# Feed-forward merging on three pairs of PSUM banks: products in groups of three instead of two

## What is computed

```python
g = mean over tokens of (relu(x @ gate_w1.T + gate_b1) @ gate_w2.T + gate_b2)     # (32, 8)
mW1 = W1 + einsum('be,efh->bfh', g, TW1)       # (32, 1024, 256): one merged matrix per batch
mW2 = W2 + einsum('be,ehf->bhf', g, TW2)       # (32, 256, 1024)
u = gelu(einsum('bsh,bfh->bsf', x, mW1) + mb1)
out = einsum('bsf,bhf->bsh', u, mW2) + mb2
x_res = x_res + tanh(g_ffn[0]) * out
```

## Time and profile before

| | |
|---|---|
| time, median of 3 runs | 1381.49 us (1380.21 to 1385.34) |
| the profiled execution: its own time | 1387.4 us |
| the profiled execution: its span | 1385.6 us |
| mean granted TensorE clock | 0.971 |
| PE busy over the span | 1304.1 us (94%) |
| DVE, ACT, POOL busy | 968.4, 678.4, 528.1 us |
| the eight chunks of stage 2 | about 154 to 518 us of the span |

### The profile page before, as it was taken

One profiled execution on the slowest core, in us unless ns is written; L12 is line 12 of the kernel. 1 busy time (PEld: TensorE's weight loads), 2 busy tenths in 40 slices (PEclk: granted clock), 3 DMA queues, 4 the chain that ended last, 5 costly groups with the idle time before them and its releaser, 6 DMA issues. The chain is left out here.

```text
span 1385.6 us, 32665 instructions
## 1 busy us (share of the span) xinstructions
PE 1304.1 (94%) x12672; PEld 924.2 (67%) x12672; DVE 968.4 (70%) x1641; ACT 678.4 (49%) x1447; POOL 528.1 (38%) x781
## 2 busy tenths in 40 slices
PE   4789999999999985999999999999998899999996
PEld 4565777877787763666777677667775575555555
DVE  7776666567656768888888888888885553454445
ACT  5854211221122124787787778877876452232220
POOL 1428888888880008333333333333320552000000
PEclk9999999999999996999999999999999699999999
DMA  8515454545451009566655556666540000000000
GB/s 222 127 42 159 133 166 135 170 135 165 134 160 42 35 4 189 94 102 101 99 93 92 91 94 102 102 100 100 93 80 2 1 1 1 14 14 26 13 13 26
DMA packets 92814, 120.28 MB, mean 87 GB/s; under 512 B 7426, under 2 KB 78939, under 8 KB 90388
## 3 DMA queue, kind: packets, MB, share of 16 engines
q1 hardware_dynamic: 83476, 87.85, 31.9%
q0 software_dynamic: 9216, 30.73, 8.2%
HBM read 96.45 MB, written 22.10 MB: 86 GB/s over the span
## 5 line engine op out<-in xcount | busy, mean ns | idle before, releaser
L1251 DVE TENSOR_REDUCE s_neg_max<-banks 112x3 bf16<-112x1461 f32 (+1 forms) x192 | 290.2, 1511 | 45.0 <-PE banks L1367 44.8
L1165 ACT ACTIVATE s_prob<-banks 128x448 f32<-128x448 f32 x512 | 272.3, 544 | 91.6 <-PE banks L1393 76.5
L702 DVE TENSOR_TENSOR s_m<-banks,s_base 128x512 f32<-128x512 f32 x256 | 161.1, 683 | 99.2 <-PE banks L856 98.9
L1393 PE MATMUL banks<-s_q_t,s_k_t 112*128 112x112 bf16 x2048 | 186.5, 215 | 1.1 <-ACT s_prob L1165 1.0
L1393 PEld LDWEIGHTS banks<-s_q_t,s_k_t 112*128 112x128 bf16 x2048 | 124.2, 98 | 72.5 <-issue 50.5
L856 PE MATMUL banks<-s_gate_sel,s_tw 64*128 64x256 f32 x1024 | 130.8, 394 | 1.6 <-DVE s_m L702 1.5
L899 PE MATMUL banks<-s_m,s_act_t 128*112 128x256 f32 x512 | 128.2, 388 | 1.5
L1409 PE MATMUL banks<-s_prob,s_v 128*32 128x112 f32 (+1 forms) x4096 | 125.8, 263 | 0.7 <-ACT s_prob L1165 0.7
L881 PEld LDWEIGHTS banks<-s_x_t,s_m 128*128 128x128 f32 x1024 | 116.7, 192 | 10.6 <-issue 7.6
L881 PE MATMUL banks<-s_x_t,s_m 128*128 128x112 f32 x1024 | 122.4, 278 | 0.0
L1890 PE MATMUL banks<-s_proj,s_weighted 128*112 128x256 f32 x512 | 115.4, 380 | 0.0
(11 more groups left out here) (271 smaller groups left out, 2340.7 us busy)
## 6 DMA issues: line engine op xcount, KB each, us to landing
k_parts<-s_k_split POOLq DMA_DIRECT2D x64, 281.2 KB, 3.7
s_k_t<-k_parts SPq DMA_DIRECT2D x32, 562.5 KB, 7.9
s_tw<-in_tw SPq DMA_DIRECT2D x16, 1024.0 KB, 5.5
s_k_raw<-in_ctx_k POOLq DMA_DIRECT2D x64, 187.5 KB, 3.8
s_k_t<-k_parts SPq DMA_DIRECT2D x32, 375.0 KB, 5.3
s_v_raw<-in_ctx SPq DMA_DIRECT2D x32, 256.0 KB
s_src<-in_ctx SPq DMA_DIRECT2D x8, 896.0 KB, 16.2
s_k_t<-k_parts SPq DMA_DIRECT2D x32, 187.5 KB, 9.1
```

The source lines that it names most:

```text
L702: nc.vector.tensor_tensor(dst[:, :, :, rows_], got, base[:, :, rows_].unsqueeze(2).broadcast_to([P, 2, B, HR]), ALU.add).then_inc(S["merge ...
L1165: nc.scalar.activation(prob[t % 2][:, c, :], w.bank(SCORE + n % SRING, P, TILE), ACT.Exp, scale=DH ** -0.5).then_inc(S["exp_done"], 1)
L1251: nc.vector.tensor_reduce(neg_max[half][:, ROWS + first:ROWS + end, 0], w.banks[0:T, MAX:MAX + end - first, 0:NKEY], AX.X, ALU.max, negate ...
L1393: last = nc.tensor.matmul(w.bank(SCORE + n % SRING)[:, s * T:(s + 1) * T], k_t[k][0:ROWS_MAX, h, c * P:(c + 1) * P], q_t[k][0:ROWS_MAX, h, :],
```

## The change

Merge units get a third pair of banks, 6 and 7, which the outputs use as well. `PAIR_OF` maps a unit to its first bank. Among `merge2` units the pairs go round in threes (0, 2, 6, 0, 2, 6, 0, 2); `merge1` units keep to 0 and 2. A `merge2` unit from the third on waits for the unit three before it. In PE's first phase the order becomes: three `merge2` units, the first products of three groups, three units, three groups, two units, two groups. Since banks 6 and 7 hold the last outputs of the chunk before, PE now waits, ahead of the merge units, until DVE has added the last pair of the chunk before (x_done). That wait stands before all units of a block of three, the first block included, and is left out in chunk 0.

```diff
@@ stage2 @@
     PAIRS = B // 2
+    PAIR_OF = (0, 2, 6)
@@ DVE @@
                     dve.wait_ge(S["merge_ps"], nth(n[0]))
                     for half in range(2):
-                        got = w.bank(2 * (n[1] % 2) + half).rearrange("p (m b r) -> p m b r", m=2, b=B)
+                        got = w.bank(n[1] + half).rearrange("p (m b r) -> p m b r", m=2, b=B)
...
-                    merged_unit((U * c + u, u), m1[:, :, :, cols], base1[:, :, cols])
+                    merged_unit((U * c + u, PAIR_OF[u % 2]), m1[:, :, :, cols], base1[:, :, cols])
...
-                    merged_unit((U * c + U1 + u, u), m2[:, :, cols].rearrange("p b (m r) -> p m b r", m=2),
+                    merged_unit((U * c + U1 + u, PAIR_OF[u % 3]), m2[:, :, cols].rearrange("p b (m r) -> p m b r", m=2),
@@ PE @@
                 def merge_unit(n, rows_):
 
-                    pe.wait_ge(S["merged"], nth(2 * (n[0] - 2) + 1))
+                    pe.wait_ge(S["merged"], nth(2 * (n[0] - n[2]) + 1))
...
-                            last = nc.tensor.matmul(w.bank(2 * (n[1] % 2) + half)[:, m * B * HR:(m + 1) * B * HR],
+                            last = nc.tensor.matmul(w.bank(n[1] + half)[:, m * B * HR:(m + 1) * B * HR],
...
-                    merge_unit((U * c + u, u), lambda m: tw1[:, u, m * P:(m + 1) * P])
+                    merge_unit((U * c + u, PAIR_OF[u % 2], 2), lambda m: tw1[:, u, m * P:(m + 1) * P])
...
-                    merge_unit((U * c + U1 + u, u), lambda m: tw2[:, 2 * u + m, :])
+                    merge_unit((U * c + U1 + u, PAIR_OF[u % 3], 2 if u < 2 else 3), lambda m: tw2[:, 2 * u + m, :])
 
                 def chunk(c, first, final):
                     for g in range(NG):
-                        if g % 2 == 0:
-                            merge2(c, g)
-                            merge2(c, g + 1)
+                        if g % 3 == 0:
+                            if not first:
+                                pe.wait_ge(S["x_done"], nth(PAIRS * c - 1))
+                            for u in range(g, min(g + 3, U2)):
+                                merge2(c, u)
                         if g == 0:
                             pe.wait_ge(S["merged"], nth(2 * (U * c + U1) - 1))
                         pe.wait_ge(S["act_done"], nth(NG * c + g - 2))
```

## The result

| | before | after |
|---|---|---|
| median of 4 runs | 1382.82 us (1380.21 to 1385.34) | 1402.05 us (1397.70 to 1406.08) |
| ratio | | 1.0126, 95% interval 1.0100 to 1.0152 |
| profiled execution, its time and span | 1387.4, 1385.6 us | 1398.5, 1396.7 us |
| stage 2, first merge to last output | 376.5 us | 392.2 us |
| one chunk of the loop, start to start | 46.12 us | 48.34 us, once 48.38 |

What follows compares the result with a forecast made beforehand. PE's own order was taken to bound stage 2's eight chunks. Terms of -3.1, +10.2 and +7.3 us summed to +14.4, added to the 1381.5 us median for 1395.9 us, 1.0% slower; range 1389.5 to 1400.5 us.

Steps and rivals of the forecast that it cites:

- How the numbers follow: Closing step: turned forecast, rivals and bounds into slower 0.89, same 0.09, faster 0.02 and the range 1389.5 to 1400.5 us.
- Part 1: First phase: one round trip between units and products less per chunk, 0.39 us each in 8 chunks, -3.1 us.
- Part 2: Chunk heads except chunk 0's: PE's first unit waits for DVE's last additions, 1.46 us each at seven, +10.2 us.
- Part 3: First block's products: group 2 waits for ACT to finish group 0, 0.91 us in all 8 chunks, +7.3 us.
- What costs nothing: Third bank pair, DVE's work on blocks of three, second phase and SP's loads were claimed to add no time.
- A: Second phase: DVE further ahead wins back 1.9 us per chunk, 15.2 us in all, giving 1380.7 us; 4%.
- B: Chunks: new gaps in PE make the clock fall, 21 us in 7 chunks, giving 1416.9 us; 6%.
- C: Only one new wait costs time: x_done's alone gives +7.1 us (1388.6), ACT's alone +4.2 us (1385.7); 8%.
- D: First phase: both waits already met and one change of kind less per chunk, giving 1378.4 us, -0.2%; 2%.

Runs made afterwards that it cites:

- the head wait alone: Kernel before plus only the x_done wait ahead of a chunk's first unit, in chunks 1 to 7; ratio to before 1.0070, +9.7 us.
- 2, 3 and 3: Three pairs of banks, blocks of 2, 3 and 3 units and groups, x_done wait in the second block; ratio to before 0.9979, -2.9 us.

## Why the prediction was right

The forecast was +14.4 us and slower; stage 2 grew by 15.7, and the ratio's interval is 13.8 to 21.0. As a time, 1395.9 us lies below the four runs' median of 1402.05, which is 1.6 us above the range's end as well; on the kernel before's 1381.49 us the ratio gives 1398.9, inside it. The distance that is left goes along with the clock outside the change: two of the four runs had the lower mean clock, and I had made no term for what the untouched stages vary by. That is the weak step in "How the numbers follow": the bounds were those of the terms alone. It also calls the range cut above, but 1400.5 is 1381.5 + 19.0, the full sum of the three upper bounds.

- **Part 1** (-0.39 us per chunk): right. A round trip is 0.38 us in blocks of one, and with one less the chunk is 0.45 shorter. The other 0.06 to 0.07 is in phase two (21.15 to 21.09 us from first to last output, in the kernels with three pairs), which I did not forecast and whose cause is open. PEld's idle of 0.33 us ahead of the products stands at each change in blocks of one too, and each costs its share of 0.38. By the reading of the Trainium skill that the prediction gave ("TensorE: Matmul & The Clock Gate", section "Step-by-step: what each phase is for"), with the loads pulled ahead over the change, blocks of one would have cost nothing; the +1.53 us per chunk does not agree with it.
- **Part 2** (+1.46 us at seven heads): right in mechanism, size off. The term that was mis-sized is "from the end of an addition to PE's load it took [...] some 0.05 us": it holds outside PE's loop (0.05 to 0.06, chunk 7 and all heads written out), but behind the new wait inside the loop it is 0.23 to 0.28. The looped heads cost 1.65 (one 1.70), chunk 1's 1.41, chunk 7's 1.46: 11.2 us instead of 10.2, just over my upper bound. I had looked for the cost of register comparisons inside phase one, where no gap shows, and not at the one place where PE stands still.
- **Part 3** (+0.91 us in eight chunks): right in mechanism, and the value was the upper bound I gave, 1.01. The wait itself is as forecast (4.59 - 3.67 = 0.92), and the group behind the gap takes 262.22 - 260.25 = 1.97 us to the next start, where the third group of a gapless block of three takes 5.54 - 3.67 = 1.87. 8.1 us.
- Together -3.5 + 11.2 + 8.1 = 15.8 us, against 15.7 found. No error of one term hid that of another by much: the parts are off by -0.4, +1.0 and +0.8.
- **What costs nothing** held: DVE finishes a block of three in 3.68 us, there is no wait on it, and the second and third x_done waits leave no gap.
- **Rivals.** A fell with the head wait alone, phase two 21.15 us both times; of its 1.9 us per chunk the changed kernel gave back 0.06 to 0.07. B fell with a clock of 1.00 in the chunks, in every kernel, though PE stood still for 1.6 us and again for 0.8 us per chunk. The swing of the clock that the Trainium skill tells of ("TensorE: Matmul & The Clock Gate", section "A second HAM failure mode: psum-queue depth-cycling") did not come about here. C and D fell with the two gaps in one trace.

## What to carry to other kernels

A wait costs from where it stands, not from where it is needed: ask of each new one what is the first instruction that needs it, put it there, and read from the trace what its releaser does at that moment. Here two units further down made 1.65 us per chunk into nothing. When work is taken from between two uses of a buffer to make longer runs, that work was also the cover for whatever refilled the buffer; sum the releaser's chain (here the first group's products, the table load and four gelus, 4.59 us from the products' start) against what is left (3.67 us). And fewer, longer runs of one kind of matmul gain only what the changes of kind cost, here 0.38 us a round trip, so both waits have to be off the path before it shows.

## What the runs showed of the hardware

- Going from 64-row products on both halves of the array to 128-row products and back costs 0.38 us at full clock, by blocks of one against two (+1.53 us for four) and by 2, 3 and 3 against four twos (-0.38 in phase one). Blocks of four save 0.35 for each of two, with up to 0.07 us of a wait in it.
- A wait at which PE stands still lets it go on 0.23 to 0.28 us behind its releaser's end inside a loop on PE, and 0.05 to 0.06 us behind it with the loop written out. It is so in the loop's first turn too.
- A table load stands at the top of each turn of ACT's loop although only one function is used in it; written out, seven of eight went, which was worth 0 where the wait was covered and 1.01 us per chunk where it was not.
- The same untouched stages behind stage 2 took 862.6 to 869.5 us in the eleven profiled executions, and the times of one kernel go along with its mean granted clock. Effects under 3 us in this kernel are read from the trace's starts, not from times.
